# A graph network pipeline on Trainium2: the attention layer's input loaded twice, and new step lists

## The reference

```python
h = relu(layernorm(x)); x = x + L0(h)   # diffusion, 8 Euler steps over adj
h = relu(layernorm(x)); x = x + L1(h)   # GAT
h = relu(layernorm(x)); x = x + L2(h)   # attention over 256 edges
h = relu(layernorm(x)); x = x + L3(h)   # Chebyshev step, masked attention with 4 heads, feed-forward
```

## Time and profile before

| what | value |
| --- | --- |
| three timed runs, median | 1242.79 us |
| lowest and highest of them | 1241.85 and 1243.12 us |
| the profiled execution: time | 1239.62 us |
| the profiled execution: span, first to last instruction | 1237.8 us |
| mean granted TensorE clock in it | 0.98 of full speed |

### The profile page before, as it was taken

The page is one execution under the profiler, slowest core; times in us unless marked ns, Lnnn a source line. Parts: engine busy times, 40 slices in busy tenths (PEclk is TensorE's granted clock), DMA queues, the critical chain, the costliest instruction groups (busy, mean ns, idle before and its releaser), DMA issues. The chain is left out here.

```text
span 1237.8 us, 23622 instructions
## 1 busy us (share of the span) xinstructions
...
## 2 busy tenths in 40 slices
...
DMA packets 123819, 83.59 MB, mean 68 GB/s; under 512 B 13296, under 2 KB 106864, under 8 KB 123760
## 3 DMA queue, kind: packets, MB, share of 16 engines
...
...
## 5 line engine op out<-in xcount | busy, mean ns | idle before, releaser
L2100 ACT ACTIVATE att_Es<-att_Ts,att_small 128x512 f32<-128x512 f32 x256 | 184.8, 722 | 61.3 <-DVE att_small L2198 60.8
L2198 DVE CUSTOM_DVE_ANT_0 att_Ts<-bank,mask_att 128x512 f32<-128x512 f32 x256 | 174.2, 682 | 33.1 <-PE bank L2356 30.6
L2410 PE MATMUL bank<-ident,att_Es 128*128 128x128 f32 x1024 | 159.7, 279 | 20.1 <-ACT att_PTs L2109 18.8
L2410 PEld LDWEIGHTS bank<-ident,att_Es 128*128 128x128 f32 x1024 | 120.9, 142 | 62.4 <-ACT att_PTs L2109 35.6
L2109 ACT COPY att_PTs<-bank 128x512 f32<-128x512 f32 x248 | 143.4, 578 | 34.4 <-PE bank L2410 33.3
L2356 PE MATMUL bank<-K_parts,Q_parts 128*128 128x512 f32 x256 | 125.1, 498 | 2.7 <-DMA K_parts<-k_lo 1.8
L1908 POOL TENSOR_SCALAR n_rs<-n_mv 128x4 f32<-128x4 f32 x46 | 14.0, 304 | 289.0 <-DVE n_mv L1903 289.0
L424 POOL TENSOR_SCALAR gat_Vs<-gat_Ts,gat_small 128x512 f32<-128x512 f32 x64 | 57.7, 916 | 81.5 <-DVE gat_small L490 81.4
L974 DVE TENSOR_TENSOR P_row<-bank,l_bias 128x512 f32<-128x512 f32 x32 | 22.1, 691 | 84.0 <-PE bank L1426 65.9
L1416 PE MATMUL bank<-G,x0T 128*128 128x128 f32 x384 | 74.8, 276 | 0.7 <-DVE U2T L967 0.5
L1416 PE MATMUL bank<-G,U1T 128*128 128x128 f32 x384 | 74.3, 275 | 0.0
...
## 6 DMA issues: line engine op xcount, KB each, us to landing
Q_parts<-q_hi SPq DMA_DIRECT2D x128, 64.0 KB, 2.0
Q_parts<-q_lo SPq DMA_DIRECT2D x128, 64.0 KB, 2.0
K_parts<-k_hi SPq DMA_DIRECT2D x128, 64.0 KB, 2.0
K_parts<-k_lo SPq DMA_DIRECT2D x128, 64.0 KB, 2.0
...
```

Of the source, the lines that this page charges most:

```text
L2100: nc.scalar.activation(att_E[:, j % RING_E, :], att_T[:, j % RING_T, :], ACT.Exp, scale=-1.0, bias=att_small[:, 0, j:j + 1], accum_out=att ...
L2198: nc.vector.tensor_tensor_reduce(att_T[:, j % RING_T, :], [c0, c1][j % 2][:], k.mask_att[:, tile_of(n, j)[1], :], -QK_SCALE, HUGE, ALU.add ...
L2410: mm = nc.tensor.transpose(dst[:, cols(s)], att_E[:, i % RING_E, cols(s)], k.ident[:])
```

## The change

GAT's input is loaded twice. A new step `load_z` loads x into zA as soon as the turn of the batch before has read zA, and raises the new semaphore gat_zloaded. `gat_stats` reads zA, `gat_apply` normalizes zA in place, and `load_x` fills xA as before, now only for the residual in `gat_x2`. All lists of steps are new; those of the loop are shown in full, those of the fill and drain shortened. Some steps now have a "+" (`ffn_final`, `att_rv`, and on SP `load_x3`, `stack0`, `stack2`, `store_out`, `edge_store`). As the number of unrolled passes, `FILL`, is worked out from the largest lag, it goes from 5 to 6: the fill's lists now hold one pass more, and the loop runs 10 times in place of 11. The drain's lists have the same passes and take in the steps that the new "+" leaves over.

```diff
     def on_sync(sp):
+        def load_z(n):
+            wait_alone(sp, sem("gat_turned"), n, sem("waits_passed"))
+            sp.dma_start(zA[:], k.nodes1(k.x1_dram, n)).then_inc(sem("gat_zloaded"), 16)
+
         def load_x(n):
...
         def gat_stats(n):
-            ready(dve, "gat_loaded", n, 16, 16)
+            ready(dve, "gat_zloaded", n, 16, 16)
             for t in range(NT):
-                nc.vector.bn_stats(g.stat[:, t, :], xA[:, t, :]).then_inc(sem("gat_stat"), 1)
+                nc.vector.bn_stats(g.stat[:, t, :], zA[:, t, :]).then_inc(sem("gat_stat"), 1)
...
         def gat_apply(n):
+            ready(dve, "gat_stat", n, NT, NT)
             ready(dve, "gat_rs", n)
             for t in range(NT):
-                nc.vector.tensor_scalar(zA[:, t, :], xA[:, t, :], g.mv[:, t, 0:1], g.rs[:, 1, t:t + 1], ALU.subtract,
+                nc.vector.tensor_scalar(zA[:, t, :], zA[:, t, :], g.mv[:, t, 0:1], g.rs[:, 1, t:t + 1], ALU.subtract,
                                         ALU.mult).then_inc(sem("gat_normed"), 1)
...
         def gat_x2(n, t0):
             if t0 == 0:
+                ready(dve, "gat_loaded", n, 16, 16)
                 ready(dve, "gat_rinv", n)
...
+                    gat["load_z"](0)
                     gat["load_x"](0)
...
+                    gat["load_z"](1)
                     gat["load_x"](1)
...
 ORDER = {
     "PE": """
-        att_score0 att_score1 att_turn15+ att_rows+ att_pv0+ att_pv1+ att_score2 att_turn0 att_score3 cheb_prop0
-        ffn_wo att_turn1 att_score4 cheb_prop1 cheb_g gat_turn att_turn2 att_score5 gat_wh ffn_turn att_turn3 gat_s2
-        ffn_up0 att_score6 ffn_up1 att_turn4 ffn_down0 att_score7 ffn_down1 att_turn5 att_score8 cheb_x1turn att_turn6
-        edge_gather0 edge_gather1 att_score9 cheb_q edge_x gat_eturn0 att_turn7 att_score10 edge_lcol att_turn8
-        edge_lb0 gat_eturn1 edge_lb1 att_score11 cheb_k att_turn9 gat_eturn2 att_score12 gat_eturn3 edge_v att_turn10
-        att_score13 edge_den gat_pv0 att_turn11 att_score14 edge_scatter att_turn12 att_score15 edge_out att_turn13
-        gat_pv1 att_turn14 cheb_v
+        att_score0 att_score1 att_turn15+ att_rows+ att_pv0+ att_pv1+ att_score2 att_turn0 att_score3 gat_turn ffn_wo
+        cheb_prop0 att_turn1 att_score4 cheb_prop1 gat_wh cheb_g att_turn2 ffn_turn att_score5 gat_s2 ffn_up0
+        att_turn3 att_score6 ffn_up1 att_turn4 att_score7 ffn_down0 ffn_down1 att_turn5 att_score8 cheb_x1turn
+        att_turn6 edge_gather0 edge_gather1 att_score9 cheb_q edge_x att_turn7 att_score10 gat_eturn0 edge_lcol
+        edge_lb0 edge_lb1 att_turn8 att_score11 gat_eturn1 cheb_k att_turn9 gat_eturn2 att_score12 gat_eturn3 edge_v
+        att_turn10 att_score13 edge_den gat_pv0 att_turn11 att_score14 edge_scatter att_turn12 att_score15 edge_out
+        att_turn13 gat_pv1 att_turn14 cheb_v
     """.split(),
     "DVE": """
-        cheb_stats cheb_aggr gat_x2a+ gat_x2b+ edge_stats att_mask0 edge_aggr att_mask1 cheb_lo gat_stats gat_aggr
-        att_mask2 att_scale att_mask3 gat_apply ffn_y2 n2_stats att_mask4 n2_aggr cheb_y n2_apply n1_stats att_mask5
-        n1_aggr gat_scores0 gat_scores1 att_mask6 gat_scores2 gat_scores3 n1_apply gat_row1 att_mask7 gat_row2 cheb_x1
-        gat_row3 ffn_y3 att_mask8 gat_max0 gat_max1 att_mask9 gat_max2 edge_z gat_max3 edge_lc att_mask10 cheb_qlow
-        edge_max0 edge_max1 att_mask11 edge_max2 edge_max3 edge_le n3_stats gat_rinv att_mask12 cheb_klow edge_rden
-        edge_attn att_mask13 edge_u n3_aggr att_mask14 n3_apply att_mask15 ffn_final edge_x3 att_rv
+        cheb_stats ffn_final+ cheb_aggr gat_x2a+ gat_x2b+ att_rv+ gat_stats gat_aggr att_mask0 edge_stats edge_aggr
+        att_mask1 gat_apply cheb_lo att_scale att_mask2 att_mask3 ffn_y2 n2_stats n2_aggr att_mask4 n2_apply cheb_y
+        n1_stats att_mask5 gat_scores0 gat_scores1 gat_scores2 n1_aggr att_mask6 gat_scores3 gat_row1 n1_apply
+        gat_row2 att_mask7 gat_row3 cheb_x1 ffn_y3 att_mask8 gat_max0 gat_max1 att_mask9 gat_max2 edge_z cheb_qlow
+        edge_lc gat_max3 att_mask10 edge_max0 edge_max1 att_mask11 edge_max2 edge_max3 edge_le n3_stats att_mask12
+        n3_aggr edge_rden att_mask13 edge_attn edge_u cheb_klow att_mask14 gat_rinv n3_apply att_mask15 edge_x3
     """.split(),
     "ACT": """
-        cheb_apply cheb_hi att_spread+ att_exp0 att_exp1 att_exp2 att_copy0 att_exp3 edge_apply cheb_xpT att_copy1
-        att_exp4 gat_hT att_copy2 edge_hi gat_wh_out0 gat_wh_out1 ffn_x2T att_exp5 att_copy3 ffn_gelu0 ffn_gelu1
-        att_exp6 att_copy4 att_exp7 att_copy5 cheb_x1T att_exp8 att_copy6 gat_exp0 edge_hg gat_exp1 edge_xz att_exp9
...
+        cheb_apply cheb_hi att_spread+ att_exp0 att_exp1 gat_hT att_exp2 att_copy0 att_exp3 edge_apply cheb_xpT
+        att_copy1 gat_wh_out0 att_exp4 edge_hi gat_wh_out1 ffn_x2T att_copy2 att_exp5 ffn_gelu0 att_copy3 ffn_gelu1
+        att_exp6 att_copy4 att_exp7 att_copy5 cheb_x1T att_exp8 att_copy6 gat_exp0 edge_hg gat_exp1 edge_xz
...
     "POOL": """
-        cheb_rstd edge_rstd ffn_res gat_rstd n2_rstd n1_rstd ffn_b2 edge_lo gat_low0 gat_low1 gat_low2 gat_low3
+        cheb_rstd gat_rstd edge_rstd ffn_res n2_rstd ffn_b2 edge_lo n1_rstd gat_low0 gat_low1 gat_low2 gat_low3
         n3_rstd
     """.split(),
     "SP": """
-        load_xr load_x3 load_x stack1+ stack3+ store_v+ load_v cheb_res stack0 stack2 edge_store store_out
+        load_z load_x3+ stack0+ stack2+ store_out+ load_xr stack1+ load_x stack3+ edge_store+ store_v+ load_v cheb_res
     """.split(),
 }
 FILL_ORDER = {
...
     "DVE": """
-        cheb_stats:0 gat_rinv:1 cheb_aggr:0 gat_x2a:1 gat_x2b:1 edge_stats:1 edge_aggr:1 cheb_lo:0 gat_stats:2
...
+        cheb_stats:0 cheb_aggr:0 gat_rinv:1 gat_x2a:1 cheb_lo:0 gat_x2b:1 gat_stats:2 gat_aggr:2 edge_stats:1
...
```

More of the change, by code:

```diff
@@ L1685 @@
-        att_turn15:0 att_rows:0 att_pv0:0 att_pv1:0 att_score2:1 att_turn0:1 att_score3:1 cheb_prop0:2 ffn_wo:0
-        att_turn1:1 gat_turn:4 att_score4:1 cheb_prop1:2 gat_wh:4 att_turn2:1 att_score5:1 gat_s2:4 cheb_g:2
-        ffn_turn:0 att_turn3:1 att_score6:1 ffn_up0:0 att_turn4:1 att_score7:1 ffn_up1:0 att_turn5:1 att_score8:1
-        ffn_down0:0 ffn_down1:0 att_turn6:1 att_score9:1 edge_gather0:3 edge_gather1:3 gat_eturn0:4 att_turn7:1
-        att_score10:1 edge_x:3 att_turn8:1 att_score11:1 cheb_x1turn:2 edge_lcol:3 gat_eturn1:4 edge_lb0:3
@@ new lines @@
+        edge_den:1 gat_eturn0:2 gat_eturn1:2 edge_scatter:1 att_score0:0 gat_eturn2:2 att_score1:0 edge_out:1
+        gat_eturn3:2 att_score2:0 att_turn0:0 gat_pv0:2 gat_pv1:2 att_score3:0 att_turn1:0 att_score4:0 cheb_prop0:1
+        cheb_prop1:1 gat_turn:3 cheb_g:1 att_turn2:0 att_score5:0 att_turn3:0 gat_wh:3 att_score6:0 gat_s2:3
+        att_turn4:0 att_score7:0 att_turn5:0 att_score8:0 edge_gather0:2 att_turn6:0 edge_gather1:2 att_score9:0
+        edge_x:2 att_turn7:0 att_score10:0 edge_lcol:2 cheb_x1turn:1 att_turn8:0 edge_lb0:2 att_score11:0 cheb_q:1
@@ new lines @@
+        gat_pv1:4 att_turn14:1 att_score0:2 att_score1:2 cheb_v:2 att_turn15:1 att_rows:1 att_pv0:1 att_pv1:1
+        att_score2:2 gat_turn:5 att_turn0:2 att_score3:2 ffn_wo:1 gat_wh:5 cheb_prop0:3 att_turn1:2 gat_s2:5
+        att_score4:2 cheb_prop1:3 ffn_turn:1 cheb_g:3 ffn_up0:1 att_turn2:2 att_score5:2 ffn_up1:1 ffn_down0:1
+        ffn_down1:1 att_turn3:2 att_score6:2 edge_gather0:4 edge_gather1:4 att_turn4:2 att_score7:2 cheb_x1turn:3
+        edge_x:4 att_turn5:2 att_score8:2 cheb_q:3 edge_lcol:4 att_turn6:2 gat_eturn0:5 att_score9:2 edge_lb0:4
@@ L1697 @@
-        gat_scores1:2 edge_max0:1 gat_scores2:2 gat_scores3:2 cheb_qlow:0 gat_row1:2 edge_max1:1 gat_row2:2 gat_row3:2
-        edge_max2:1 edge_max3:1 cheb_klow:0 edge_le:1 gat_max0:2 gat_max1:2 edge_rden:1 gat_max2:2 edge_attn:1
-        edge_u:1 gat_max3:2 att_mask0:0 att_mask1:0 edge_x3:1 cheb_stats:1 cheb_aggr:1 att_mask2:0 att_mask3:0
-        gat_rinv:2 gat_x2a:2 gat_x2b:2 edge_stats:2 cheb_lo:1 att_mask4:0 edge_aggr:2 att_mask5:0 gat_stats:3
-        gat_aggr:3 att_mask6:0 gat_apply:3 cheb_y:1 n1_stats:1 att_mask7:0 n1_aggr:1 att_mask8:0 n1_apply:1
@@ new lines @@
+        edge_rden:1 edge_attn:1 edge_u:1 gat_rinv:2 att_mask0:0 att_mask1:0 edge_x3:1 cheb_stats:1 cheb_aggr:1
+        att_mask2:0 gat_x2a:2 gat_x2b:2 gat_stats:3 cheb_lo:1 gat_aggr:3 edge_stats:2 att_mask3:0 edge_aggr:2
+        gat_apply:3 att_mask4:0 cheb_y:1 n1_stats:1 att_mask5:0 n1_aggr:1 att_mask6:0 gat_scores0:3 gat_scores1:3
+        att_mask7:0 gat_scores2:3 gat_scores3:3 att_mask8:0 gat_row1:3 n1_apply:1 gat_row2:3 gat_row3:3 cheb_x1:1
+        att_mask9:0 edge_z:2 att_mask10:0 gat_max0:3 edge_lc:2 gat_max1:3 edge_max0:2 att_mask11:0 gat_max2:3
@@ new lines @@
+        edge_max1:2 gat_max3:3 cheb_qlow:1 att_mask12:0 edge_max2:2 edge_max3:2 att_mask13:0 edge_le:2 att_mask14:0
+        cheb_klow:1 edge_rden:2 edge_attn:2 gat_rinv:3 edge_u:2 att_mask15:0 att_rv:0 edge_x3:2 cheb_stats:2 gat_x2a:3
```

(14 more changed lines are left out.)

235 lines of the change are left out of this document (122 added, 113 removed).

## The result

The changed kernel takes 1224.52 us (median of 4 runs, 1224.07 to 1226.01) where the kernel before, beside it, took 1242.32 (4 runs, 1241.63 to 1243.12): a ratio of 0.9859, interval 0.9841 to 0.9876. It is faster by 17.8 us; 1223 was forecast. In two later comparisons the same changed kernel had medians of 1224.28 and 1225.26 and ratios of 0.983 (0.981 to 0.985) and 0.983 (0.980 to 0.987), because the kernel before was slower there (medians 1245.6 and 1245.2).

A forecast was written before the change was run, and what follows sets the result against it. Bound: a chain changing engines, with ScalarE's run started late behind VectorE's DMA wait. Per pass 0.5 + 1.0 + 0.2 = 1.7 us; 17 + 2 + 1 = 20; 1239.6 - 20 plus 3.2 is 1223 us, range 1212 to 1239.

The forecast's parts named there:

- ScalarE's run: First half of a loop pass: gat_hT moves into ScalarE's idle time before att_exp2, 1.0 us gained a pass.
- What it gives back: Moved att_copy2 and att_copy3: a 1.0 us hole at att_turn4 replaces 1.10 at ffn_down0; no loss, bounds 0 and 0.5.
- The DMA term: Start of a loop pass: jitter from VectorE's wait for the input load goes, 0.5 us a pass (0.2 to 0.6).
- second half of the pass: Loop from att_turn6 on: small swaps of steps gain 0.2 us a pass (bounds -0.5 and 0.5).
- The pass that moved into the fill: Batch 1 to 2, now in the fill list with the new order in its first half: 2 us gained.
- Start of the layers: Before the loop: cheb_lo placed after the first half of gat_x2, 1 us gained (0 to 2.5).
- Rest of the fill and drain: Same steps reordered outside the loop: 0, bounds 3 us either way.
- A: Rival: only the DMA jitter goes, ScalarE's run does not set the loop's period; 5 us gained, 1238; chance 0.14.
- B: Rival: SP's queue becomes the bound, K parts reach the loop's scores late; slower, 1250; chance 0.07.
- C: Rival: a grown TensorE hole lowers its granted clock in the loop, taking 19 us back, 1242; chance 0.03.
- D: Rival: the new fill and drain lists are worse and take back all the gain, 1242; chance 0.04.
- E: Rival: more goes, TensorE's holes in the loop close too, 2.6 us a pass, 1212; chance 0.06.

The follow-up runs named there:

- e4: Changed kernel with gat_turn, gat_wh, gat_hT and gat_wh_out0 put back at their late places in the loop's lists; 1238.81 us.
- e11: Changed kernel with gat_hT, gat_wh_out0 and gat_wh put back late in the loop's lists, gat_turn left early; 1236.22 us against 1225.26.
- e7: Kernel before with the second copy, its load at the head of SP's list, other lists as before; 1240.28 us against 1245.62.
- e2: Changed kernel with both the fill and the drain lists of the kernel before; 1226.86 us.
- e3: Kernel before with the second copy and its waits alone, all other lists as before; 1242.92 us against 1246.37.
- e12: Kernel of e7 with only the GAT steps moved forward in the loop's lists; 1257.32 us against 1245.9 of the kernel before.
- e1: Changed kernel with the drain lists of the kernel before; 1222.94 us.
- e5: Changed kernel run again, nothing edited; 1224.28 us.
- e9: Changed kernel run again as a control, nothing edited; 1225.26 us.
- e8: Changed kernel with att_copy3 ahead of ffn_gelu0 in ScalarE's loop list; 1226.72 us.

## Why the prediction was right, point by point

The mechanism was right in the loop: the steps came where they were drawn and the period is as forecast. That the total came within 2 us of the forecast is in part luck. The 20 us of gain were worked out against one trace of before; between the two traces it is 13.6, between the medians beside each other 17.8, and in the two later comparisons 21.3 and 20.0.

- **The loop, 1.7 us a pass, period 45.6.** Measured 1.64 and 45.49, in every pass. The sum was right; its split was not confirmed. Its bounds of 0.6 and 2.4 do not follow from the terms' own, which add to 0.2 and 2.1.
- **"ScalarE's run", 1.0 us net of "What it gives back".** The undoing costs 1.44 (e4), of which 1.18 hang on `gat_hT`, `gat_wh` and `gat_wh_out0` (e11) and 0.26 on `gat_turn`; up to 0.45 of it is the wait that the undoing made, so against the old lists the term is 1.0 to 1.4. The steps came as drawn, counted from the pass's `att_rows`: `gat_turn` 5.5 us behind it (forecast 823.9 - 818.4 = 5.5; measured 813.74 - 808.27), `gat_hT` 6.1 (6.1) and `att_exp2` 6.6 (6.6). The hole at `att_turn4` was put at 1.0 us and is 1.36. What the sum left out is that `ffn_wo` and `cheb_g` no longer wait; it said that they pay only if ScalarE keeps up, and took nothing for them. In e4 and e11 `cheb_g` waits 0.7 us again.
- **"The DMA term", 0.5.** The traces give 0.1 (47.13 to 47.0 in e7), the medians up to 0.5, and e7 pays for an added wait for K parts. That the wait is gone was right, and that `ffn_wo`'s wait goes with it too; how much that shortens a pass is open. All that is not the four moves is worth 47.13 - 46.93 = 0.20 by the trace of e4, this term and the other swaps ("second half of the pass": 0.2 taken) together, where the prediction had 0.7 for both. The prediction held 2.6 us by the Trainium skill, "DMA: Bandwidth & Descriptors", section "Anatomy of one DMA — SWDGE (gpsimd) path", against the measured 3.75 and said that the trace disagrees; as said above, that fit is for transfers that GpSimd issues, so it does not bear on this load.
- **"The pass that moved into the fill", 2 us, and "Start of the layers", 1 us.** From batch 1's mark to batch 2's it is 46.6 us instead of 48.3: 1.7. The first matmul of `cheb_prop` starts at 458.76 instead of 461.82, 3.06 us earlier, of which 1.25 is an earlier front part (`gat_x2a` at 457.50 against 458.75) and 1.8 the new order, as worked out. But nothing of it is left at batch 0's mark: 534.43 against 534.84, and in the seven later traces with the new fill lists and both copies 534.3 to 536.9, with the old fill lists (e2, e3, e7, e12) 533.5 to 535.5. This term was 0 or less rather than 1. The three passes from there to batch 3's mark took 137.4 instead of 142.1 us, 4.7 less.
- **Rest of the fill and drain, 0 ±3.** Not refuted: the fill gives 1 to 4 us (partly counted above), the drain takes 0 to 2.
- **A** fell with the period of 45.49. **B**: the last K part of `stack1` was issued 6.3 us behind `att_rows` instead of 5.9, yet no score waited for one in the nine passes; e7 shows that the wait is near. **C**: the clock was 1.00 in the loop. **D** seemed to hold at first sight, 5.7 us lost in the last stretch of the two traces; e1, e5 and e9 show that most of this was the chance of the two executions. **E**: the holes did not close; one of 1.36 and one of 0.52 us remain at `att_turn4` and `att_turn5`, and e8 could not remove them.
